# End of a unit: convolutions ahead of low parts on DVE, tap and gate activation ahead of a square and a weight tile on ACT

## The reference, cut to what matters

```python
proj = jnp.einsum('bsd,ed->bse', x, in_proj_w)
gate = proj[..., :INTER]
hBC = silu(causal_conv4(proj[..., INTER:INTER + CONV_DIM]) + conv_b)
...
Y = (Y_diag + Y_off).reshape(b, s, H, P) + hs * D[None, None, :, None]
g = y * jax.nn.silu(gate)
gg = g.reshape(b, s, G, INTER // G)
var = jnp.mean(gg * gg, axis=-1, keepdims=True)
gg = gg * jax.lax.rsqrt(var + EPS)
out = gg.reshape(b, s, INTER) * norm_w
return jnp.einsum('bsi,oi->bso', out, out_proj_w)
```

## Time and profile before

| | |
|---|---|
| runs | 1787.37, 1789.04, 1789.48 us; median 1789.04 |
| the profiled execution's own time | 1789.48 us |
| its span, first to last instruction | 1787.7 us |
| mean granted TensorE clock | 0.992 |
| busy in a 1787.7 us span | PE 97%, PEld 76%, DVE 77%, ACT 60%, POOL 55% |

### The profile page before, as it was taken

The page is one execution under the profiler, slowest core; times in us unless marked ns, Lnnn a source line. Parts: engine busy times, 40 slices in busy tenths (PEclk is TensorE's granted clock), DMA queues, the critical chain, the costliest instruction groups (busy, mean ns, idle before and its releaser), DMA issues.

```text
span 1787.7 us, 31728 instructions
## 1 busy us (share of the span) xinstructions
PE 1730.7 (97%) x9798; PEld 1353.3 (76%) x9798; DVE 1380.6 (77%) x2269; ACT 1076.4 (60%) x1826; POOL 977.0 (55%) x732
## 2 busy tenths in 40 slices
PE   6899999999999999999999999999999999999998
PEld 4667778777777777777787777777777777877766
DVE  4777788777877788777887778777887778886786
ACT  6566565666656666565556665566575656566554
POOL 1545564655546575355646555465653647565662
PEclk9899999999999999999999999999999999999999
DMA  6412121111212121021211212121221212212211
GB/s 231 115 28 74 57 74 45 49 57 55 75 33 71 51 70 55 27 74 57 68 51 36 65 56 80 29 74 43 64 62 34 68 51 77 74 51 68 68 48 59
DMA packets 80936, 112.97 MB, mean 63 GB/s; under 512 B 28402, under 2 KB 32498, under 8 KB 79988
## 3 DMA queue, kind: packets, MB, share of 16 engines
q1 hardware_dynamic: 62898, 78.24, 15.0%
q10 hardware_dynamic: 17858, 32.52, 5.4%
HBM read 88.42 MB, written 22.29 MB: 62 GB/s over the span
## 4 chain that ended last, share of the span: by engine, by line
issue 46%; POOL 36%; PE 11%; DVE 3%; ACT 3%; POOLq 1%; DMA 1%; SPq 0%; ACTq 0%; DVEq 0%
POOL yt L1858 10%; POOL ssq L1852 7%; POOL prev L1834 6%; POOL wg_lo L1759 4%; POOL wo_lo L1759 3%; PE bank L518 3%; POOL yt L1861 3%; POOL wx_lo L1759 3%; PE bank L520 2%; PE bank L519 2%; PE bank L779 1%; DMA gate<-w_mod_dram 0%; PE bank L909 0%; PE bank L697 0%; POOL acc L1779 0%
## 5 line engine op out<-in xcount | busy, mean ns | idle before, releaser
L1858 POOL TENSOR_TENSOR yt<-yt,ea 128x384 f32<-128x384 f32 (+1 forms) x126 | 186.4, 1479 | 375.1 <-DVE ea L1642 375.1
L1610 DVE TENSOR_TENSOR lm<-lm,cbm 128x512 f32<-128x512 f32 x256 | 190.0, 783 | 146.0 <-ACT lm L1192 145.2
L1405 DVE SCALAR_TENSOR_TENSOR xc<-bank,bpar,xc 128x511 f32<-128x511 f32 (+2 forms) x384 | 285.5, 743 | 6.8
L518 PE MATMUL bank<-h_hi,wg_hi 128*128 128x512 f32 x640 | 262.4, 410 | 18.1 <-ACT gate L1117 8.1
L520 PE MATMUL bank<-h_hi,wg_lo 128*128 128x512 f32 x640 | 251.2, 393 | 0.0
L519 PE MATMUL bank<-h_lo,wg_hi 128*128 128x512 f32 x640 | 250.7, 392 | 0.0
L518 PE MATMUL bank<-h_hi,wx_hi 128*128 128x512 f32 x512 | 211.8, 414 | 4.1 <-DVE bt L1405 2.2
L1834 POOL TENSOR_TENSOR prev<-prev,dec 128x512 f32<-128x512 f32 x96 | 129.8, 1352 | 156.3 <-DVE prev L1551 91.4
L518 PE MATMUL bank<-wo_hi,g_hi 128*128 128x512 f32 x496 | 206.3, 416 | 0.0
L520 PE MATMUL bank<-h_hi,wx_lo 128*128 128x512 f32 x512 | 201.6, 394 | 0.0
L519 PE MATMUL bank<-h_lo,wx_hi 128*128 128x512 f32 x512 | 200.5, 392 | 0.0
(11 more groups left out here) (238 smaller groups left out, 3956.3 us busy)
## 6 DMA issues: line engine op xcount, KB each, us to landing
raw_w<-w_in_dram SPq DMA_DIRECT2D x145, 256.0 KB, 2.7
raw_w<-w_out_dram SPq DMA_DIRECT2D x64, 256.0 KB, 2.6
part_d<-part ACTq DMA_DIRECT2D x64, 256.0 KB, 2.1
part<-part_d ACTq DMA_DIRECT2D x60, 256.0 KB, 2.7
rt<-rows_d SPq DMA_DIRECT2D x256, 6.0 KB
acc<-x_dram SPq DMA_DIRECT2D x8, 256.0 KB, 6.7
acc<-w_mod_dram SPq DMA_DIRECT2D x2, 1024.0 KB, 6.2
lh<-neg_d SPq DMA_DIRECT2D x128, 6.0 KB
```

The source lines that it names most:

```text
L518: nc.tensor.matmul(out_ap, whi(k), hhi(k), start=(k == 0), stop=False)
L1405: stt(dst[:, at], ps[:, 0:HALF - 3 + k], w(k), dst[:, at], ALU.mult, ALU.add)\
L1610: tt(lm[:, h % 4, :], lm[:, h % 4, :], cbm[:, toks(hf)], ALU.mult).then_inc(v_m, 1)
L1858: tt(y[:, cols], y[:, cols], ea_tile(end, j)[:, cols], ALU.add).then_inc(p_t3, 1)
```

## The change

In a unit's second half, at j >= 2, DVE makes the convolutions of step j ahead of lower_g(j - 1). At j == 3 ACT rounds g tile 2, taps x tile 3, then squares g tile 2, activates the next unit's gate tile 0 (not at c = 3), and only then takes the weight tile and the silus. `split_g` is cut into `round_g` and `square_g`. The last unit (`end`, not `more`) keeps its order.

```diff
--- before.py
+++ after.py
@@ -1199,7 +1199,7 @@
                         se.wait_ge(t_ss, 2 * GROUPS - 1)
                     act(ea_tile(not more, j), bank[ea_bank(c, j)][:, :], ACT.Copy).then_inc(a_ea, 1)
 
-                def split_g(j):
+                def round_g(j):
 
                     se.wait_ge(p_g, 4 * u + j + 1)
                     if j == 0:
@@ -1211,8 +1211,10 @@
                             se.wait_ge(d_scr, 16 * 20)
                     y = yt_tile(not more, j)
                     act(g_parts(not more)[0][:, j, :], y, ACT.Copy, scale=par(c // 2, j, NORM)).then_inc(a_hi, 1)
-                    if j == NCT - 1 and not (last and c == 3):
-                        silu_x(u + 1, 3)
+
+                def square_g(j):
+
+                    y = yt_tile(not more, j)
                     if c < 2 and j == 0:
                         ge(se, t_ss, 2 * g - 1 + hf)
                     elif more or j == 0:
@@ -1222,6 +1224,12 @@
                     else:
                         se.wait_ge(t_yo, 4 * u)
                     act(ssq[:, hf, :] if c < 2 and j == 0 else sq_tile(not more, j), y, ACT.Square).then_inc(a_sq, 1)
+
+                def split_g(j):
+                    round_g(j)
+                    if j == NCT - 1 and more:
+                        silu_x(u + 1, 3)
+                    square_g(j)
 
                 def ffn_signs(i):
 
@@ -1246,7 +1254,9 @@
                             if j == 2:
                                 split_g(0)
                             exp_a(j + 1)
-                    if j >= 1 and more:
+                    if j == 3 and more:
+                        round_g(2)
+                    elif j >= 1 and more:
                         split_g(j - 1)
                     elif j == 2:
                         split_g(1)
@@ -1259,6 +1269,10 @@
                             ge(se, d_bpar, 16 * (nv + 1))
                         tap(item, item_bank(n), nv, hv, g + 1, pv)
                         n += 1
+                    if j == 3 and more:
+                        square_g(2)
+                        if c < 3:
+                            silu_gate(u + 1, c + 1, 0)
                     for f in todo[j:j + 1]:
                         if first and j == 0:
                             se.wait_ge(d_scr, 16 * 20)
@@ -1270,8 +1284,6 @@
                                 silu_b(g + 1)
                             silu_x(u + 1, 0)
                         else:
-                            if c < 3:
-                                silu_gate(u + 1, c + 1, 0)
                             silu_x(u + 1, 1)
                             silu_x(u + 1, 2)
                             if c == 3:
@@ -1640,11 +1652,13 @@
                     ve.wait_ge(a_ea, 4 * u + j + 1)
                     e = ea_tile(end, j)[:, cols]
                     tt(e, bank[yo_bank(end, j)][:, cols], e, ALU.mult).then_inc(v_t1, 1)
-                    if j >= 1 and not end:
-                        lower_g(j - 1)
+                    if j == 1 and not end:
+                        lower_g(0)
                     for item in items[j]:
                         conv(item, item_bank(n), nv, hv, g + 1, pv)
                         n += 1
+                    if j >= 2 and not end:
+                        lower_g(j - 1)
                 if end:
                     lower_g(0)
                     lower_g(1)
```

## The result

The changed kernel takes 1829.2 us (median of 4 runs, 1826.02 to 1831.9) against 1789.26 for the kernel before in the same comparison: ratio 1.0223, 95% interval 1.0204 to 1.0243. It is 40 us slower, where 22.4 were forecast; the sign was right, and the size lay 4 us above the end of the range. The profiled execution took 1828.63 us, its span is 1826.8.

A forecast was written before the change was run, and what follows sets the result against it. TensorE, busy 97% of the span, was taken as the bound, so only its waits count. 16 x 1.15 + 8 x 0 + 5 x 0.8 = +22.4 us gave 1811.4 us against 1789.04; range 1792 to 1825.

The forecast's parts named there:

- The gate order gains nothing: At c=0 to 1, TensorE's wait for the gate activation isn't removed but grows by about 0.2 us.
- low(1) makes yt(3) late: At c=0 to 1, low(1) falls into the middle of POOL's square sum, and yt(3) starts 0.65 us late.
- low(2) and low(3) stand back to back with a POOL instruction between them: At c=0 to 1, both wait for POOL behind convolution 3; low(3) ends at 75.95 instead of 74.68.
- output projection 0 waits for low(3): At c=0 to 1, TensorE starts it at 76.0 instead of 74.82, +1.15 us.
- The rival "as meant": Port waits don't chain, the gate wait goes, 24 handovers gain 0.44 us each: 1778.5 us; chance 0.13.
- 1.6 us per handover: Estimate with whole instructions excluded on the port: low parts end at about 76.4, total near 1819 us.
- the term of c=1 to 2: Low(1) and POOL's square sum nearly coincide; DVE taken to go first, 0 us, bounds -0.4 and +1.3.
- The rival with this term: POOL goes first at c=1 to 2: another 8 x 1.3 = 10.4 us, 1821.8; chance 0.17.
- 1.15 us at the 16 others: Handovers c=0 to 1 and c=2 to 3 in 8 groups each lose 1.15 us, 18.4 in all.
- 5 x 0.8 = 4.0 us at the loop's return: At c=3 to 0, ACT's square behind the tap delays the next gate by 0.8 us at five returns.
- the mixed rival: One handover kind gains 0.44, another loses 1.15, loop's return costs 0 to 4: +2 to +11 us; chance 0.14.

The follow-up runs named there:

- run 1: The changed order on DVE alone, ACT as in the kernel before: 1828.69 us, ratio 1.0227.
- run 2: The changed order on ACT alone, DVE as in the kernel before: 1788.32 us, ratio 1.0000.
- run 3: The changed kernel with low(2) again ahead of convolution 3, so only low(1) stands behind its convolution: 1800.49 us, ratio 1.0063.
- run 4: The changed kernel with low(1) again ahead of convolution 2, so only low(2) stands behind its convolution: 1796.45 us, ratio 1.0042.
- run 5: The changed kernel with POOL's square sums and second-half weight lowerings cut to one column in the loop's six groups: 1774.17 us, 0.992 of before.
- run 6: The kernel before with POOL's square sums and second-half weight lowerings cut to one column in the loop's six groups: 1765.48 us, ratio 0.9873.
- run 9: The kernel of run 4 plus a one-column POOL memset ahead of the square sum of tile 2 at c=0: 1790.25 us, ratio 1.0003.
- run 10: The changed kernel plus a one-column POOL memset ahead of the square sums of tiles 1 and 2 at c=1: 1819.49 us, ratio 1.0177.

## Why the prediction had the chain right, one term wrong and its size short

**Right.** The gate order gains nothing, low(1) makes yt(3) late, low(2) and low(3) stand back to back with a POOL instruction between them, and output projection 0 waits for low(3): rows and runs 1 to 6 show each. The rival "as meant" falls: its point of decision, convolution 3 ending ahead of POOL's multiply, is reached in run 4 (and with the memset in runs 9 and 10), and in run 4 the order costs nothing in two of three kinds of handover, but gains nothing either. The rule of the Trainium skill, page "SBUF — State Buffer", section "Who interferes with whom" (the port is held for the whole instruction), would by the prediction's estimate have given 1.6 us per handover, nearer to the 1.58 and 1.55 measured than my 1.15; but the ends of the low parts still lie 0.55 after POOL's, as I had them, so its number is right for other reasons, below.

**Wrong: the term of c=1 to 2.** "I take 0, because the DVE request is queued on a running instruction." This was the step that failed. The starts were forecast to 0.02 us, and POOL won. This is the handover in the changed kernel's timeline of DVE and POOL:

```profile
1036.84 1.84 DVE L1629 SCALAR_TENSOR_TENSOR g_lo<-yt,bpar,g_hi 128x512 fp32r<-128x512 f32 x1
1036.86 1.27 POOL L1866 TENSOR_TENSOR ssq<-ssq,sq 128x512 f32<-128x512 f32 x1
```

Low(1) starts first, 1.84 us long; the square sum behind it isn't stretched. The same happens to low(2) six microseconds later. The term measured 8 x 1.66 = 13.3 us. Run 10 shows by the memset that the order of the two decides it: where DVE goes first, 0.15 of the 1.66 us are left. In groups 0 and 7 POOL's square sum even starts 0.04 to 0.05 us ahead of low(1)., on which I leaned, has DVE 0.36 us ahead, which says nothing of a tie. The rival with this term had chance 0.17 and 1.3 us per handover.

**Mis-sized: 1.15 us at the 16 others**, which measured 1.58 and 1.55, 6.6 us more in sum. Two pieces are seen. yt(3) uses the buffer of yt(1), so it waits for low(1)'s semaphore; with low(1) right in front it starts at 988.97, 0.13 after that one's end of 988.84, where I had let it start 0.08 before, as neighbours without such a wait do. Those 0.2 us pass through ea(3) to POOL's add, which waited for it (0.27 idle), to the square sum and so to both low parts. The second is at the end: output projection 0 starts 0.14 after low(3), where I had 0.05. The last 0.1 or so of the 0.4 wasn't followed up.

**Mis-sized the other way: 5 x 0.8 = 4.0 us at the loop's return**, which came to 0.7 in all. ACT's last instruction is late there as forecast, but the gate isn't. ACT's timeline after, against the earlier trace rows:

```profile
939.89 0.62 ACT L1226 ACTIVATE sq<-yt 128x512 f32<-128x512 f32 x1
942.01 0.60 ACT L1117 ACTIVATE gate<-bank 128x512 f32<-128x512 f32 x1 [1.50 <-issue]
```

| | POOL's square sum of tile 2 ends | ACT's branch | ACT's last square ends | gate starts |
|---|---|---|---|---|
| before, third return | 9.81 | 9.91 | 10.47 | 12.80 |
| after, third return | 9.88 | 9.98 | 11.25 | 12.74 |
| after, fourth return | 10.42 | 10.52 | 11.24 | 13.48 |
| run 9, third return | 9.37 | 9.47 | 10.74 | 12.14 |

The last wait of ACT's loop body is that of the square of tile 3 for POOL's square sum of tile 2 (L1221 of the changed kernel). 0.10 us after that square sum ends (0.15 in run 6) the sequencer branches, while the engine still works off what it was given, and the gate starts 2.61 to 3.05 us after the branch, at all 60 returns of the twelve traces; behind ACT's last instruction the distance is anything from 0.80 to 2.45. So a later last instruction of ACT is hidden by the return, and what moves the gate is POOL. The branch is 0.07 us later than before at four returns of the changed kernel. At the fourth it is 0.6 late: there low(2) of c=3 won its tie, POOL's square sum behind it lasted 1.84 instead of 1.30 us, and the gate came 0.7 later than at the other four. In run 1 this is so at four of the five returns. A tie that DVE wins, which is a gain at c=0 and 1, is a loss at c=3.

In sum: 18.4 + 0 + 4.0 = 22.4 forecast; 25.0 + 13.3 + 0.7 = 39.0 measured. Had the tie been called the other way, with the prices left as forecast, the sum would have been 18.4 + 10.4 + 4.0 = 32.8. The range failed because its upper end took the forecast's unit prices as bounds. (The upper end of the mixed rival, +11, doesn't come out of its numbers: 8 x (1.15 - 0.44) + 4.0 is 9.7. Nothing else rests on it.)

## What to carry to other kernels

Moving a short instruction behind a long one on DVE isn't free of POOL: where DVE reads two SBUF tensors, ask what POOL runs at the new place. Above all look at two such instructions in a row in front of a wait of TensorE: what they cost hung on how far the first one led POOL's next instruction. With a lead of 0.47 and 0.65 us the pair cost nothing (run 4, c=2 to 3 and 1 to 2), with 0.03 us it cost 1.2. A wait that stands first in the list (8.1 us for the gate here) is worth only the distance to the next one behind it; read the ends of all the producers that the bound engine meets in the next few microseconds before moving one. At a hardware loop's return count from the last wait of the body, not from the engine's last instruction. And a start of such a DVE instruction that a timeline puts within 0.05 us of POOL's next one is a tie: price both outcomes into the forecast and the range, with everything that chains behind them.

## What the hardware showed that I had not expected

- The loser of a tie can be the one that started first. Over all traces of this study I took the low parts, multiplies and xw_lo that began while a POOL instruction ran with another right behind it (memsets not counted, and not the one-column instructions of runs 5 and 6, where the durations don't tell who went first). With a lead of DVE on that next one of under 0.02 us, POOL went first in 16 of 16; from 0.02 to 0.04 in 37 of 39; from 0.04 to 0.06 in 10 of 34; above 0.06 in none of more than 380. All those below 0.06 us are low parts, at places that repeat from group to group, so they are few distinct situations.
- A one-column memset of 0.10 us on POOL, run between the two, took 6 us off a kernel in which it turned five such ties (run 9) and 9 to 10 off one in which it turned six (run 10). It lay beside the low part without holding it up.
- ACT's sequencer returns to the head of the loop while the engine still works. In this kernel ACT's gate starts 2.61 to 3.05 us after its sequencer's branch at all 60 returns, whatever ACT's last instruction does: 2.33 us idle with ACT early, 1.50 with it 0.8 us later. The branch follows the last wait of the loop body, here for POOL.
